# Mixing the residual streams with block matrices in (token, stream) layout, and a Sinkhorn split of three samples and five

## The reference

```python
x_norm = x * rsqrt(mean(x * x) + RMS_EPS)              # x is y here
H_res = sinkhorn_log(x_norm @ W_res.T + H_res_base)    # 4x4 per token, 50 iterations, tau 0.1
H_pre, H_post = softmax(...), softmax(...)             # 4 per token each
g = sigmoid(gate)[0]
H_res = (1.0 - g) * I + g * H_res
x_streams = x.reshape(B, T, 4, 256)
x_pre = einsum('btnc,btn->btc', x_streams, H_pre)
y = x_pre @ W_branch
x_mixed = einsum('btij,btjc->btic', H_res, x_streams)
y_distributed = einsum('btc,btn->btnc', y, H_post)
return x_mixed + y_distributed
```

## Time and profile before

| what | value |
|---|---|
| median of the runs | 874.49 us |
| profiled execution | 874.75 us |
| its span, first to last instruction | 872.8 us |
| TensorE busy | 761.2 us (87%) |
| VectorE busy | 578.2 us (66%) |
| ScalarE busy | 335.4 us (38%) |
| mean of a 128x512 matmul of the base product (line 947) | 0.40 us |
| VectorE's iterations of group 1 | 750.0 to 836.6 us |
| last mixing and stores | 836.6 to 872.8 us |

### The profile page before, as it was taken

The page is one execution under the profiler, slowest core; times in us unless marked ns, Lnnn a source line. Parts: engine busy times, 40 slices in busy tenths (PEclk is TensorE's granted clock), DMA queues, the critical chain, the costliest instruction groups (busy, mean ns, idle before and its releaser), DMA issues.

```text
span 872.8 us, 11055 instructions
## 1 busy us (share of the span) xinstructions
PE 761.2 (87%) x3172; PEld 488.5 (56%) x3172; DVE 578.2 (66%) x2036; ACT 335.4 (38%) x577; POOL 64.7 (7%) x34
## 2 busy tenths in 40 slices
PE   4989899989899999998968899999898892699656
PEld 2544444344444444444645788887687771587445
DVE  6555282434675656483746524438999998899998
ACT  0333733304534252434324633444333421757152
POOL 0002000202621011022020000000000000000000
PEclk9999999989999999999999899999999996899969
DMA  8994654133448353512031345334333249653103
GB/s 340 374 334 163 240 179 171 60 111 140 159 149 355 108 189 139 193 56 89 24 121 50 129 161 182 115 114 159 122 128 108 102 155 411 272 193 121 48 35 158
DMA packets 40297, 140.94 MB, mean 161 GB/s; under 512 B 8511, under 2 KB 9663, under 8 KB 34626
## 3 DMA queue, kind: packets, MB, share of 16 engines
q1 hardware_dynamic: 38962, 137.72, 43.8%
q10 hardware_dynamic: 1296, 2.74, 0.8%
HBM read 106.86 MB, written 33.58 MB: 161 GB/s over the span
## 4 chain that ended last, share of the span: by engine, by line
PE 49%; DVE 34%; ACT 8%; issue 5%; DMA 2%; POOL 1%; DVEq 0%; SPq 0%; ACTq 0%
PE PS L779 21%; PE PS L837 12%; PE PS L947 8%; DVE ksum L1361 6%; DVE kprod L1356 6%; DVE ka L1365 4%; DVE nr L1438 4%; DVE kb L1365 3%; PE PS L826 2%; ACT qT L542 2%; DVE xr L1283 2%; PE PS L868 2%; DMA x_raw<-x_tr_dram 2%; PE PS L794 1%; DVE xp L1268 1%
## 5 line engine op out<-in xcount | busy, mean ns | idle before, releaser
L779 PE MATMUL PS<-w_raw,x_raw 128*128 128x512 f32 x512 | 230.4, 604 | 13.7 <-DMA x_raw<-x_tr_dram 11.0
L779 PEld LDWEIGHTS PS<-w_raw,x_raw 128*128 128x128 f32 x512 | 96.7, 194 | 124.9 <-issue 124.1
L947 PE MATMUL PS<-w_hi,xT_hi 128*128 128x512 f32 x256 | 105.0, 410 | 0.0
L947 PE MATMUL PS<-w_lo,xT_hi 128*128 128x512 f32 x256 | 102.0, 399 | 0.0
L947 PE MATMUL PS<-w_hi,xT_lo 128*128 128x512 f32 x256 | 101.7, 397 | 0.0
L1361 DVE TENSOR_REDUCE ksum<-kprod 128x16 f32<-128x64 f32 x392 | 75.2, 233 | 0.2 <-issue 0.2
L837 PE MATMUL PS<-w3q,qT 128*128 128x512 bf16 x256 | 61.3, 395 | 14.4 <-ACT qT L542 14.4
L1131 DVE SCALAR_TENSOR_TENSOR gbuf<-PS,lnst,vecs 128x512 f32<-128x512 f32 x32 | 23.7, 749 | 75.0 <-PE PS L837 75.0
L542 ACT ACTIVATE qT<-PS,round_c 128x512 bf16<-128x512 f32 x64 | 40.3, 679 | 84.4 <-PE PS L826 84.3
L837 PE MATMUL PS<-w1q,qT 128*128 128x512 bf16 x256 | 60.4, 391 | 8.4 <-DVE x1buf L1149 5.7
L470 POOL TENSOR_TENSOR xres<-xres,vecs 128x1024 f32<-128x1024 f32 x16 | 42.2, 2659 | 329.8 <-DMA xres<-x_tok_dram 329.8
(11 more groups left out here) (165 smaller groups left out, 1128.2 us busy)
## 6 DMA issues: line engine op xcount, KB each, us to landing
w_raw<-cond_w_dram SPq DMA_DIRECT2D x32, 1024.0 KB, 5.6
stage<-w_dram SPq DMA_DIRECT2D x16, 512.0 KB, 12.1
x_raw<-x_tr_dram SPq DMA_DIRECT2D x32, 256.0 KB, 6.4
xres<-x_tok_dram SPq DMA_DIRECT2D x8, 1024.0 KB, 9.3
x_scratch<-x1buf SPq DMA_DIRECT2D x16, 512.0 KB, 6.4
x1n<-x_scratch SPq DMA_DIRECT2D x16, 512.0 KB, 5.7
xr<-x_scratch SPq DMA_DIRECT2D x16, 512.0 KB, 3.6
y_scratch<-y SPq DMA_DIRECT2D x16, 512.0 KB, 3.6
```

The costliest lines, as they stand in the source:

```text
L779: mm = pe.matmul(PS[:, 2 * t + h, :], x_raw[pr][:, c, t * P:(t + 1) * P], w_raw[pr][:, c, h * H2:(h + 1) * H2], start=(pr == 0 and c == 0) ...
L947: pe.matmul(PS[:, 2 * t + h, :], xx[:, c, t * P:(t + 1) * P], ws[c // 2][:, c % 2, h * H2:(h + 1) * H2], start=(c == 0 and xx is xT_hi and ...
```

## The change

1. The groups are samples 0 to 2 (6 tiles, chains of 3) and 3 to 7 (10 tiles, chains of 5). Group 0 starts before step 3 and has shares of 3, 3, 2, 2 iterations in each of steps 3 to 7 (the last share is 1).
2. Each iteration's column half reads a transposed copy of the matrix, `kmat_t`, so that its product and its sum run over neighbouring elements. The start makes the copy with two more instructions.
3. `distribute`, `load_xr` and `store_r` are gone. ScalarE copies the branch out of PSUM (`evac_branch`) and keeps it for all samples.
4. y and x1 are loaded for mixing in another layout: partition t*4+r holds stream r of token t, for four groups of 32 tokens in turn. Rows of a transfer are 1 KB long. There H_res of 32 tokens is one 128x128 matrix with 4x4 blocks, so a tile takes 4 matmuls instead of 16. `select` and `pick` bring H_res in this layout (four matmuls, two products, one sum a group).
5. H_post times the branch becomes four more matmuls a tile (`rest_part`), with matrices `post` that ScalarE makes from the identity.
6. Behind step 7, TensorE first does `rest_part` of four tiles of group 1 (AHEAD = 4), then group 0's mixing, then `rest_part` of the other six. Behind the last iteration each of the ten tiles takes one block set (7 by VectorE, 3 by ScalarE), four matmuls, and one VectorE addition of 128x1024; then it is stored.
7. Loops over steps and iterations are written out.

```diff
-    GROUP = NT // 2
-    HG = GROUP // 2
+    FIRST = 3
+    N0 = FIRST * NTOK
+    N1 = NT - N0
+    TILES = (N0, N1)
+    HG = (N0 // 2, N1 // 2)
-    BY_DVE = 5
+    BY_ACT = (2, 4, 6)
+    AHEAD = 4
...
+            def streams(a):
+                return a.rearrange("(j t) (r c) -> (t r) j c", j=NS, r=NS)
...
             sp.wait_ge(l1_done, 4 * NB)
-            for i in range(GROUP - NTOK):
-                load_last(i)
+            for i in range(N1):
+                load_last_x(i)
             store_y(NB - 1)
-            store_r(NB - 1)
+            for i in range(N1 - NTOK):
+                load_last_y(i)
...
+            def rest_part(n, tile, xs, done):
...
                 for h in range(2):
-                    pe.matmul(PS[:, b + h, :], ident[:, :], rs[:, h * H2:(h + 1) * H2], start=True, stop=False)
+                    pe.matmul(PS[:, 2 * (n % 2) + h, :], ident[:, :], xs[:, 2 * h:2 * h + 2, :].rearrange("p j c -> p (j c)"),
+                              start=True, stop=False)
+                pe.wait_ge(post_done, n + 1)
+                pe.wait_ge(br_ev, tile // NTOK + 1)
+                pt = post[n % 2][:, :, :].rearrange("p t q -> p (t q)")
+                for j in range(NS):
+                    mm = pe.matmul(region(n, j), pt[:, j * P:(j + 1) * P],
+                                   br[:, tile // NTOK, (tile % NTOK) * C:(tile % NTOK + 1) * C], start=False, stop=(done and j % 2 == 1))
...
-                    nc.vector.tensor_tensor(kprod[i][:, :, :, :], kmat[i][:, :, :, :], cols(v, HG) if row else rows(v, HG),
+                    nc.vector.tensor_tensor(kprod[i][:, 0:hg, :, :], (kmat if row else kmat_t)[i][:, 0:hg, :, :], cols(v, hg),
                                             ALU.mult).then_inc(k_step[i], 1)
...
-                        n = B_ITERS // 4
-                        iterations(0, (b - NB // 2) * B_ITERS + i * n, n)
+                        iterations(0, (b - FIRST) * B_ITERS + (0, 3, 6, 8)[i], 1 if last and i == 3 else (3, 3, 2, 2)[i])
...
-                if not first:
-                    distribute(b - 1)
...
             sinkhorn_start(1)
-            with dve.Fori(0, (SINKHORN - 1) // 7) as it:
-                iterations(1, it * 7, 7)
+            pick(0)
+            iterations(1, 0, SINKHORN - 1)
             sinkhorn_finish(1)
...
+            def last_add(i):
+
+                dve.wait_ge(fm_done, i + 1)
+                nc.vector.tensor_tensor(nr[i][:, :, :].rearrange("p (b j) c -> p b (j c)", b=2),
+                                        PS[:, 2 * (i % 2):2 * (i % 2) + 2, :],
+                                        nr[i][:, :, :].rearrange("p (b j) c -> p b (j c)", b=2), ALU.add).then_inc(f_add, 1)
+
+            pick(1)
+            dve.wait_ge(hs_step, 4)
+            last_block(0)
+            last_block(1)
+            for i in range(N1):
+                if i + 2 < N1 and i + 2 not in BY_ACT:
+                    last_block(i + 2)
+                last_add(i)
```

More of the change, by code:

```diff
@@ L487, in lora_lo @@
                                         ALU.subtract).then_inc(a_lo, 1)
-            with pool.Fori(0, NB) as b:
+            for b in range(NB):
                 lora_lo(b)
@@ L701, in step_b @@
                 square(b, 0)
+                if not first:
+                    evac_branch(b - 1)
                 if not last:
@@ L1030, in _ @@
             x_transposes(1, 1)
-            step_b(1)
-            with pe.Fori(2, NB - 1) as b:
+            for b in range(1, NB - 1):
                 step_b(b)
@@ new lines, in rest_part, with mix_part, select @@
+                if done:
+                    mm.then_inc(pm_done, 1)
+            def mix_part(n, k):
+                pe.wait_ge(blk_done, k + 1)
+                for j in range(NS):
+                    mm = pe.matmul(region(n, j), blk[k % BLK][:, j, :, :].rearrange("p t q -> p (t q)"), my[k % MIX][:, j, :],
+                                   start=False, stop=(j % 2 == 1))
+                mm.then_inc(pm_done, 1)
+            def select(g):
+                pe.wait_ge(sel_set, 1)
+                pe.wait_ge(sk_step, SK_OPS * (g + 1))
+                if g == 0:
+                    pe.wait_ge(xl_done, 4 * NB)
+                else:
+                    pe.wait_ge(br_ev, NB)
+                w = TILES[g] * NR
+                for j in range(NS):
+                    mm = pe.matmul(PS[:, SEL_BANK + 2 * g + j // 2, (j % 2) * w:(j % 2 + 1) * w],
+                                   sel[:, j * TQ:(j + 1) * TQ, :].rearrange("p t q -> p (t q)"),
+                                   hres[g][:, :, :, :].rearrange("p t q r -> p (t q r)"), start=True, stop=True)
+                mm.then_inc(hs_mm, 1)
@@ new lines, in last @@
+            def last(i):
+                if i in BY_ACT:
+                    pe.wait_ge(ablk_done, BY_ACT.index(i) + 1)
+                else:
+                    pe.wait_ge(nblk_done, i + 1 - sum(a < i for a in BY_ACT))
+                pe.wait_ge(ny_ld[i], 16)
+                if i < 2:
+                    pe.wait_ge(pm_ev, NT)
+                else:
+                    pe.wait_ge(f_add, i - 1)
+                for j in range(NS):
+                    mm = pe.matmul(region(i, j), blk[i % BLK][:, j, :, :].rearrange("p t q -> p (t q)"), ny[i][:, j, :],
+                                   start=True, stop=True)
+                mm.then_inc(fm_done, 1)
@@ new lines, in _ @@
+            for i in range(AHEAD):
+                pe.wait_ge(nx_ld[i], 16)
+                rest_part(i, N0 + i, nr[i], True)
+            select(0)
+            for k in range(N0):
+                pe.wait_ge(my_ld[k % MIX], 32 * (k // MIX + 1))
+                rest_part(AHEAD + k, k, mr[k % MIX], False)
+                mix_part(AHEAD + k, k)
+            for i in range(AHEAD, N1):
+                pe.wait_ge(nx_ld[i], 16)
+                rest_part(N0 + i, N0 + i, nr[i], True)
+            select(1)
@@ L1065, in _ @@
+            for i in range(N1):
+                last(i)
         @block.vector
@@ L1350, in half @@
-            def half(k, row):
-                vec, new = (kb, ka) if row else (ka, kb)
+                    nc.vector.tensor_tensor(kmat_t[i][:, 0:hg, :, :].rearrange("p t j i -> p t i j"), hr[:, chain[g][i], :, :],
+                                            cols(sa[:, 1, chain[g][i], :], hg), ALU.mult).then_inc(k_step[i], 1)
                 for i in range(2):
-                    v = vec[i][:, :, :]
+                    nc.vector.memset(kb[i][:, 0:hg, :], 1.0).then_inc(k_step[i], 1)
+            K0 = 3 + K_OPS * (SINKHORN - 1) + 1
@@ L1355, in half @@
+            def half(g, k, row):
+                vec, new, hg = *((kb, ka) if row else (ka, kb)), HG[g]
+                for i in range(2):
+                    v = vec[i][:, 0:hg, :]
                     dve.wait_ge(k_step[i], k)
-                    nc.vector.tensor_tensor(kprod[i][:, :, :, :], kmat[i][:, :, :, :], cols(v, HG) if row else rows(v, HG),
+                    nc.vector.tensor_tensor(kprod[i][:, 0:hg, :, :], (kmat if row else kmat_t)[i][:, 0:hg, :, :], cols(v, hg),
                                             ALU.mult).then_inc(k_step[i], 1)
```

328 lines of the change are left out of this document (163 added, 165 removed).

## The result

The changed kernel takes 860.25 us (median of four runs, 857.1 to 861.76); the kernel before, beside it, 874.51. The ratio is 0.983, with a 95% interval of 0.980 to 0.986. The forecast was -7.1 us; it came to -14.3. The direction was right, the time lies inside the range given, and the gain is twice the forecast.

A forecast was written before the change was run, and what follows sets the result against it. VectorE was taken to bound steps with iterations and the stretch behind step 7, TensorE most of the rest. Terms of -12.8, -1.5, +2.5, +1.9, +6.7 and -3.9 us sum to -7.1: median 867.4 us, range 859 to 877.

The forecast's parts named there:

- Terms 1 and 2: Steps with iterations fall to TensorE's pace, -12.8 us; ScalarE's wait at the head of sample 7 goes, -1.5 us.
- The lower clock: In steps with iterations, TensorE's clock drops after its wait for VectorE's gather; a 128x512 matmul takes 0.63 us, mean 0.40.
- term 2: Head of sample 7: ScalarE's root no longer waits 1.51 us for VectorE's first instruction of the last softmaxes, -1.5 us.
- Term 3: From the last gather to group 1's exponential: ScalarE reaches it only behind three `rest_part` copies, +2.5 us.
- Term 4: Group 1's start gets longer: ten tiles for eight, two more instructions for `kmat_t`, and `pick(0)`, +1.9 us.
- Term 5: Group 1's 49 iterations of ten tiles: 1.90 us each in place of 1.71, loop cost gone, +6.7 us.
- the two terms of 0.07: Per iteration with chains of 5: four products 16 elements longer, +0.07 us, and four sums the same, +0.07 us.
- The terms for `kmat_t`: Per iteration of group 1: the column sum reads neighbouring elements in place of a stride, -0.08 us.
- The rival of latency: Group 1's iterations: chain latency sets a stage, half the growth counts, 1.77 us each, -0.1 in all; 861 us; chance 0.13.
- Term 6: Last mixing and stores behind the iterations: 32.3 us in place of 36.2, with 1 KB packets at 55 to 60 ns, -3.9 us.
- the two prices weighed there: Last stores' 1 KB rows: skill's rule, 7% more than 4 KB rows; small-packet row, about 23 ns a packet beside the bytes.
- the signs that the prediction named for being wrong: 1 KB packets over 80 ns, steps over 33 us, or a stall over 18 us would each make it wrong.

The follow-up runs named there:

- the last version: Changed kernel with group 1's exponentials ahead of the copies, groups of four samples and four, a step's twelve iterations shared 3, 4, 3, 2: 837.76 us, ratio 0.955.

## Why the prediction was right in its direction and wrong in its size

- **Terms 1 and 2, right** (-14.6 for -14.3). Steps with iterations were bound by VectorE and fell to TensorE's own pace; the run with less `distribute` shows the bound. What the changed kernel's shorter steps owe to each part of the change is not measured; the last version reaches 30.8 us with twelve iterations a step, so moving iterations out was not needed. The lower clock, which the prediction put beside the wait, cost these steps little. ScalarE's root no longer waits in sample 7 (707.82, no idle time before it), as term 2 had it.
- **Term 3, right** (+2.6 for +2.5). The added stall was where the text put it, 14.9 us long where it said about 13; moving the exponential ahead gives it back.
- **Term 4, nearly right** (+1.5 for +1.9).
- **Term 5, wrong in size** (+1.6 for +6.7). This is the step that failed: "four reciprocals 4 elements longer at 8 ns, +0.13", and beside it the two terms of 0.07. The fifth tile costs 0.175 us an iteration and not 0.27, and 49 x 0.095 = 4.7 us are nearly all of the miss. By stage, a reciprocal's grows by 0.033 us where 0.064 was charged, a product's by 0.021 where 0.038 was, a sum's by 0.034 where 0.038 was. The slopes came from a pair's duration at one end and a lone instruction's at the other. Between pair rows a reciprocal goes from 227 ns (16 elements) to 242 (20), a product from 217 to 227, a sum from 211 to 226; each charged twice a stage, as the prediction did, they give 0.030, 0.020 and 0.030, or 0.16 an iteration. So the mixed slopes suffice to explain the miss. That both instructions of a pair were charged isn't shown to be an error: for the strided sum it is what happens, and for reciprocals the runs fit 4 ns twice as well as 8 ns once. The terms for `kmat_t` (-0.08; -0.09 with four tiles, -0.11 with five) and for the loop (-2.6; 2.1 to 2.7) held.
- **The rival of latency** had 1.77 and -0.1 us for the term, and 861 us in all; measured are 1.80, +1.6 and 860.25. It lies nearer than the forecast, but partly by luck. Its price was worked out from the same mixed slopes, and with slopes between lone rows its rule gives 0.12 for the fifth tile, too little; the strided sum speaks against it too. Its total came out because the 1.7 us that its term lacks are made up by the other rows of the ledger, 1.2 us of them scatter. What the forecast brought against it, that products and sums are 0.27 us apart, "just two instructions' throughput", does not hold either: with one chain they are 0.27 apart as well (736.78 to 737.05).
- **Term 6, right** (-4.8 for -3.9). Packets of 1 KB took 47 ns where 55 to 60 were forecast, and the end came 3.5 us behind the last addition and not 4.5. The stores did not bind. Of the two prices weighed there, the Trainium skill's rule (DMA: Bandwidth & Descriptors, Why small descriptors are slow) gives 7% more for 1 KB rows and the row with small packets some 60%; the 19% measured lie between, nearer to the rule.
- The other 2.6 us between the profile's -14.8 and the forecast are the start of the program (-1.2, scatter), the tail (-0.9), the start of group 1 (-0.4) and the steps (-0.3), less 0.1 in term 3. All but the last have the same sign as the miss in term 5. None of the signs that the prediction named for being wrong (packets over 80 ns, steps over 33 us, a stall over 18 us) came; all three would have shown a slower kernel, and it had none for a faster one.

What stays open: why a pair's stage grows as it does. Taking the second instruction away saved 0.014 us a stage (0.08 / 6) at five tiles, but no run varied the length of one chain alone, so the runs don't say whether a reciprocal's elements are paid once or twice.

## What to carry to other kernels

Take a price per element only between rows in the same situation, pairs with pairs and lone instructions with lone ones, and in chains that take turns read it from start to start of a whole stage. Before work is added behind an in-order engine's wait, look at what stands behind it in that queue: here three copies ahead of one small exponential cost as much as the whole change gained. Before a lower clock of TensorE is charged as a cost, look at which engine sets the pace there: in steps bound by VectorE it cost at most 0.6 us of 35, in a stretch bound by TensorE nearly 2.
